# Reordering four small places of the schedule of a fused attention and feed-forward layer: rotation, low parts, reciprocals and one split wait

## The reference

```
n = layernorm(x)
q, k, v = n @ w_q, n @ w_k, n @ w_v
lk = (n @ w_lq) @ w_lk;  lv = n @ w_lv          # one latent key and value head for each query head
q, k, lk = rope(q), rope(k), rope(lk)
x = x + causal_softmax(q k) v @ w_o + causal_softmax(q lk) lv @ w_lo
n = layernorm(x)
x = x + n @ W.T + b + 2 * sum_e routing[e] * (n @ A[e].T) @ B[e].T
```

## Time and profile before

| what | value |
|---|---|
| median of 3 runs | 2029.95 us (2029.53 to 2030.79) |
| the profiled execution, its own time | 2030.6 us |
| its span, first to last instruction | 2028.8 us |
| granted TensorE clock | 0.999 of full speed |
| busy: PE, PEld, DVE, ACT, POOL | 2016.4, 1751.1, 1456.7, 1204.7, 891.0 us |

### The profile page before, as it was taken

One profiled execution on the slowest core, in us unless ns is written; L12 is line 12 of the kernel. 1 busy time (PEld: TensorE's weight loads), 2 busy tenths in 40 slices (PEclk: granted clock), 3 DMA queues, 4 the chain that ended last, 5 costly groups with the idle time before them and its releaser, 6 DMA issues.

```text
span 2028.8 us, 33417 instructions
## 1 busy us (share of the span) xinstructions
PE 2016.4 (99%) x11716; PEld 1751.1 (86%) x11716; DVE 1456.7 (72%) x2884; ACT 1204.7 (59%) x2505; POOL 891.0 (44%) x684
## 2 busy tenths in 40 slices
PE   8999999999999999999999999999999999999999
PEld 7888888888888888888888888888888888888887
DVE  7777776776777767777677776777767776777777
ACT  4666556665665655666565665666556665666561
POOL 5444544445443454444534444444544435444422
PEclk9999999999999999999999999999999999999999
DMA  3211111111111121111111111211111111120131
GB/s 107 49 34 44 44 32 36 37 47 40 33 44 32 40 44 37 44 28 49 32 42 35 39 38 34 49 33 41 45 34 33 39 44 42 29 49 23 38 69 42
DMA packets 101797, 83.78 MB, mean 41 GB/s; under 512 B 28152, under 2 KB 73848, under 8 KB 101632
## 3 DMA queue, kind: packets, MB, share of 16 engines
q1 hardware_dynamic: 101632, 81.65, 16.1%
HBM read 79.26 MB, written 2.36 MB: 40 GB/s over the span
## 4 chain that ended last, share of the span: by engine, by line
PE 98%; DVE 1%; ACT 0%; issue 0%; DMA 0%; SPq 0%; DVEq 0%; ACTq 0%
PE bankT L596 13%; PE scores L523 12%; PE scores L524 12%; PE scores L525 12%; PE bankX L523 9%; PE bankX L525 9%; PE bankX L524 9%; PE bankO L525 7%; PE bankO L524 7%; PE bankO L523 7%; PE scores L562 0%; DMA stage<-in_L_attn_w_q 0%; ACT probs L891 0%; DVE probs L1124 0%; DVE probs L1108 0%
## 5 line engine op out<-in xcount | busy, mean ns | idle before, releaser
L830 ACT ACTIVATE PT_hi<-bankT 128x512 fp32r<-128x512 f32 (+2 forms) x640 | 337.6, 533 | 304.4 <-PE bankO L525 269.2
L1130 DVE TENSOR_TENSOR PT_lo<-bankT,PT_hi 128x512 fp32r<-128x512 f32 (+2 forms) x640 | 388.6, 607 | 171.8 <-ACT PT_hi L830 169.3
L891 ACT ACTIVATE probs<-probs,nmax 128x128 f32<-128x128 f32 (+7 forms) x512 | 394.5, 773 | 129.8 <-DVE nmax L1124 129.6
L1124 DVE CUSTOM_DVE_ANT_0 probs<-scores,mask 128x128 f32<-128x128 f32 (+7 forms) x512 | 379.3, 750 | 68.8 <-PE scores L525 67.4
L596 PE MATMUL bankT<-ident,probs 128*128 128x128 f32 x2304 | 380.9, 274 | 2.4 <-DVE PT_lo L1130 1.7
L596 PEld LDWEIGHTS bankT<-ident,probs 128*128 128x128 f32 x2304 | 278.8, 140 | 63.5 <-DVE PT_lo L1130 12.3
L1388 POOL TENSOR_TENSOR rot<-rot,cos 128x512 f32<-128x512 f32 x144 | 187.1, 1299 | 257.0 <-DVE rot_half L1141 257.0
L1382 POOL TENSOR_TENSOR OT_lo<-o_raw,OT_hi 128x512 fp32r<-128x512 f32 x63 | 98.7, 1566 | 314.1 <-ACT OT_hi L830 314.1
L830 ACT ACTIVATE OT_hi<-o_raw 128x512 fp32r<-128x512 f32 x128 | 146.7, 1146 | 140.0 <-DVE o_raw L1199 140.0
L1390 POOL TENSOR_TENSOR rot<-rot,rot_half 128x512 f32<-128x512 f32 x144 | 199.8, 1387 | 11.3
L1140 DVE TENSOR_TENSOR rot_half<-rot,sin 64x512 f32<-64x512 f32 x144 | 100.1, 695 | 136.2 <-ACT rot L830 133.2
(11 more groups left out here) (310 smaller groups left out, 5334.5 us busy)
## 6 DMA issues: line engine op xcount, KB each, us to landing
inv_b<-inverses SPq DMA_DIRECT2D x128, 256.0 KB, 3.9
stage<-in_L_attn_w_q SPq DMA_DIRECT2D x32, 256.0 KB, 4.9
stage<-in_L_attn_w_lv SPq DMA_DIRECT2D x32, 256.0 KB, 2.8
stage<-in_L_attn_w_o SPq DMA_DIRECT2D x32, 256.0 KB, 3.5
stage<-in_L_attn_w_lo SPq DMA_DIRECT2D x32, 256.0 KB, 2.6
acc<-in_L_attn_hidden_states SPq DMA_DIRECT2D x8, 256.0 KB, 4.9
stage<-in_L_attn_w_k SPq DMA_DIRECT2D x8, 256.0 KB, 5.2
stage<-in_L_attn_w_v SPq DMA_DIRECT2D x8, 256.0 KB, 5.4
```

The costliest lines, as they stand in the source:

```text
L830: return act.activation(place, src, ACT.Copy)
L891: act.activation(prob_tile(c, t), prob_tile(c, t), ACT.Exp, bias=nmax[:, c, t:t + 1], scale=-1.0, accum_out=rsum[:, c, t:t + 1]).then_inc( ...
L1124: dve.tensor_tensor_reduce(place, src, tile_view(mask[:, S - width:S], c), -SCALE, -MASKED, ALU.add, ALU.min, nmax[:, c, t:t + 1]).then_in ...
L1130: dve.tensor_tensor(pt_place(1, hh, w, j), bankT[j % 2][:, block_columns(c, j):CH], f32(pt_place(0, hh, w, j)), ALU.subtract).then_inc(pt_ ...
```

## The change

Four edits. On VectorE, the rotation of Q half 1 moves from the end of slot 0 of window 3 to the end of slot 1, behind the low part of one more block; and in windows with c = 0 the reciprocals come behind the row maximum of the first tile instead of ahead of it. On GpSimd, `ropes` (used for LK) makes the low part of half 0 ahead of the product and sum of half 1; before, both sums came first, except in the very last head. On TensorE, OUT0 waits for `Wo` and the ordinary half, does three matmuls, and only then waits for `Wlo` and the latent half, where it waited for the later ones ahead of all six.

```diff
@@ TensorE
-            def out_tile(c, i, bank=0):
+            def out_half(c, i, bank, kind):
                 rows = slice((TPC * c + i) * P, (TPC * c + i + 1) * P)
-                mm3(banksX[bank], both(OT, ALL, 0, rows), both(Wo, ALL, ALL), True, False)
-                return mm3(banksX[bank], both(OT, ALL, 1, rows), both(Wlo, ALL, ALL), False, True)
+                return mm3(banksX[bank], both(OT, ALL, kind, rows), both((Wo, Wlo)[kind], ALL, ALL), kind == 0, kind == 1)
                 elif name == "OUT0":
+                    pe.wait_ge(w_lo, load_no(g, hh, "Wo") + 1)
+                    pe.wait_ge(o_lo[0], n_out_low(g, hh, 0))
+                    out_half(0, n, bank, 0)
                     pe.wait_ge(w_lo, load_no(g, hh, "Wlo") + 1)
                     pe.wait_ge(o_lo[0], n_out_low(g, hh, 1))
-                    mm = out_tile(0, n, bank)
+                    mm = out_half(0, n, bank, 1)
                 else:
                     pe.wait_ge(o_lo[1], n_out_low(g, hh, 0) - 1)
-                    mm = out_tile(1, n, bank)
+                    out_half(1, n, bank, 0)
+                    mm = out_half(1, n, bank, 1)
@@ VectorE
+            def invert_sums(g, hh, w):
+
+                dve.wait_ge(exped, tiles_made(g, hh, w))
+                dve.reciprocal(rinv[:, WINDOWS[w][1], :], rsum[:, WINDOWS[w][1], :]).then_inc(inverted, 1)
                     for s in range(BLOCKS[w]):
-                        if s == 0:
-                            dve.wait_ge(exped, tiles_made(g, hh, w))
-                            dve.reciprocal(rinv[:, c, :], rsum[:, c, :]).then_inc(inverted, 1)
+                        if s == 0 and c == 1:
+                            invert_sums(g, hh, w)
                                     row_max(tiles_made(g, hh, w) + t, t % 2, WINDOWS[nw][1], t)
+                                    if c == 0 and t == 0:
+                                        invert_sums(g, hh, w)
                         here = pieces_of(g, hh, w)
-                        behind = here.get(s, ("", 0)) == ("Q", 1)
-                        if s in here and here[s][0] != "LK" and not behind:
+                        if s in here and here[s] != ("Q", 1) and here[s][0] != "LK":
                             piece(g, hh, w, s, *here[s], piece_bank(g, hh, w, s))
                         if s + 2 < BLOCKS[w]:
                             block_lo(g, hh, w, s + 2)
-                        if behind:
-                            piece(g, hh, w, s, *here[s], piece_bank(g, hh, w, s))
+                        if here.get(s - 1, ("", 0)) == ("Q", 1):
+                            piece(g, hh, w, s - 1, *here[s - 1], piece_bank(g, hh, w, s - 1))
@@ GpSimd
             def ropes(g, hh, name, places, at):
                 for n in range(2):
                     rope_add(rope_no(g, hh, name, n), rope_no(g, hh, name, n) % RING, n)
-                for n in range(2):
                     rope_low(rope_no(g, hh, name, n), rope_no(g, hh, name, n) % RING, places, at(n))
-                    if w == 0 and not more:
-                        for n in range(2):
-                            no = rope_no(g, hh, "LK", n)
-                            rope_add(no, no % RING, n)
-                            rope_low(no, no % RING, LKT, (ALL, chunk(n)))
-                    elif w == 0:
+                    if w == 0:
                         ropes(g, hh, "LK", LKT, lambda n: (ALL, chunk(n)))
```

## The result

| | before | changed |
|---|---|---|
| median of the runs | 2030.09 us (2029.53 to 2030.79, 4 runs) | 2017.41 us (2016.83 to 2018.19, 4 runs) |
| ratio | | 0.9938, 95% interval 0.992 to 0.9955 |
| span of the profiled execution | 2028.8 us | 2015.3 us |

What follows compares the result with a forecast made beforehand. TensorE's matmul stream was taken to bound the kernel (98% of the chain). 5.3 + 2.5 + 1.7 + 4.1 - 0.7 = 12.9 us off 2030.6 gives 2017.7, the median 0.65 lower: 2017.1 us; own range 2014.5 to 2020, stated range 2014 to 2023.5.

Steps and rivals of the forecast that it cites:

- a: GpSimd's low part of LK half 0 ahead of half 1's product and sum: TensorE's wait on `LKT_lo` goes, 5.3 us gained.
- b: VectorE's reciprocals behind the first row maximum: the maximum comes 0.08 us sooner in 31 heads, 2.5 us gained.
- c: TensorE's split wait of OUT0: the 0.07 us stall on `OT_lo` goes in 24 heads, 1.7 us gained.
- d: VectorE's rotation of Q half 1 behind a low part in window 3: 0.17 us in 24 heads, 4.1 us gained.
- stalls only move: Rival: TensorE, once faster, meets the next late operand; at most 2 to 4 us gained, 2027 us; chance 0.09.
- the rival of their price: Rival: OUT0's "issue" time is the price of waits, so 256 new ones cost 20 us, 2039 us; chance 0.06.
- group ends: At 7 group ends the later rotation delays the addition of OUT0 0 and stalls OUT0 1: 0.1 us each, 0.7 lost.
- The rival built on it: Rival: VectorE 0.4 us later stalls block 6's transposes in window 3; d brings nothing, 2021.9 us; chance 0.25.

Runs made afterwards that it cites:

- the earlier row maximum: Changed kernel with group ends as before, plus the row maximum of window 2's first tile taken ahead of block 1's low part: 2015.04 us.
- The four single runs: Each takes one of the four edits alone into the kernel before: a 2024.16, b 2027.44, c 2029.51, d 2026.21 us.

## Why the prediction was right

**a.** Forecast 5.3 us, measured 5.3 alone and 0.19 and 0.16 us a head in the changed kernel. Each sub-step is in the rows: `LKT_lo` 2.4 us earlier, the second one in its place, `OT_lo` longer by 0.18 for a forecast of 0.2, at no cost.

**b.** Forecast 2.5, measured 2.0. The mechanism was right. 0.08 us sooner on VectorE gave TensorE 0.06 to 0.07 us. The whole stall had been read as 0.10 us: what the swap won and what the earlier row maximum won behind it, 0.07 and 0.04 us, come to 0.11.

**c.** Forecast 1.7 as a term of its own. It is 1.6 with d and 0.0 without. The sum came out because d was in it; the step that was wrong is treating the term as free of its neighbour. I had both stalls in the same fence, 2.7 us apart, and did not ask whether the second one was fixed in time by VectorE. It was: a low part behind the rotation is ready when VectorE has made it, and TensorE arriving 0.08 us sooner waits 0.08 us longer. The rival "stalls only move" was right for this one edit by itself, and wrong for the others. The waits themselves cost nothing that shows in the run that repeats them; the rival of their price fell.

**d.** Forecast 4.1 less 0.7 at group ends, 3.4 together; measured 3.3 alone. The loss at a group end was 0.14 to 0.15 us, inside the bounds of 0 to 0.2, larger than the 0.1 I took. That it is the rotation's is shown by the run that leaves it in slot 0 there. The profile names no wait there, but the starts of matmuls show it where the prediction had put it: at OUT0 1, whose bank the addition of OUT0 0 frees 0.05 us ahead of the late start.

**The lock.** The rotation met `QT_lo` as worked out, 0.16 us behind it for 0.13, and took 1.68 us. Here the trace agrees with what the Trainium skill, page "SBUF — State Buffer", section "Who interferes with whom", states: a VectorE operation with two inputs in SBUF and a GpSimd operation that reads SBUF shut each other out. The rival built on it needed VectorE 0.4 us later than worked out. It was not, but the room was thin: 0.12 us in the 17th head (1066.58 to 1066.70) for 0.2 worked out. The run with one instruction of 0.48 us more used it up and cost 6.9 us, more than the 4.1 + 0.7 of the rival: the rival had left c its gain, and that goes with d's.

**Sum.** 12.9 us forecast and 12.7 measured (12.7 again on the second chip). The four single runs add up to 10.6, and with c taken as it is beside d to 12.2; the rest is within what the times can tell. In the trace a head that does not end a group is 0.52 us shorter, for 0.49 forecast. That the sum is so close owes something to luck: c was kept only by d, and small misses cancelled: b came out 0.5 us under its term and the group ends lost 0.3 us more, while c and d gave 0.26 us a head for 0.24.

## What to carry to other kernels

On an engine that is busy 99% of the time, look for the waits of its weight loads, and price them by the distance of matmul starts there against a clean stretch: 0.35 us of wait was 0.16 to 0.19 us of loss. Before adding up such stalls, ask of each what fixes the moment its operand is ready: if another engine's own order fixes it, a gain just ahead of it is given back in full, so remove the later stall of a pair first. When a step is moved back on one engine, follow it to the engine that waits for it in order; what stands behind that wait there is what the move puts at risk.

## What the runs showed that I had not expected

Waits on TensorE that are long satisfied cost nothing that shows, even eight at a time between matmuls of 0.23 us, and 1024 of them made only 512 instructions. A late operand costs less than its wait until the lead is used up: weight loads with 0.21 us of idle time ahead of them cost 0.04 us, those of OUT0 with 0.23 us 0.07, those with 0.28 us about 0.10, those with 0.35 us 0.16 to 0.19, and the transposes' with 0.39 and 0.45 us cost 0.19 and 0.26. In every case the loss is the idle time less 0.16 to 0.20 us. And moving a rotation by one slot helped by 3.3 us while moving it by one more cost 15.3, because the engine that it made late was another one.
